# Reordering the steps of a hand-scheduled Mamba-2 decoder layer: conv tile one ahead of the gate, decays multiplied a step later

## The reference, cut to what matters

```python
proj = jnp.einsum('bsd,od->bso', h, in_proj_w)      # gate 8192, hid 8192, B 1024, C 1024, dt 128
hBC  = silu(causal_conv(hBC, conv_w, conv_b))        # 4 taps, on hid, B and C
...
Y_diag = einsum('bcijh,bcjhp->bcihp', (C.B) * L, hid*dt)   # L: exp of sums of A*dt, causal
y  = (Y_diag + Y_off) + D*hid
yg = y * silu(gate)
y  = yg * rsqrt(mean(yg*yg over the group) + EPS) * gnorm_w
out = residual + y @ out_proj_w.T
...
q1 = fake_quant(layernorm(x)); q2 = fake_quant(ctx); x = x + q1 @ q2
x = x + ffn(layernorm(x)[:, perm])[:, unperm]
```

## Time and profile before

| | us |
|---|---|
| median of 3 runs | 943.29 (942.54 to 943.3) |
| profiled execution, its own time | 941.07 |
| profiled execution, its span | 939.3 |
| PE busy | 821.1 (87%) |
| DVE busy | 696.5 (74%) |
| POOL busy | 624.8 (67%) |
| ACT busy | 542.9 (58%) |
| mean granted TensorE clock | 0.933 |

### The profile page before, as it was taken

One profiled execution on the slowest core, in us unless ns is written; L12 is line 12 of the kernel. 1 busy time (PEld: TensorE's weight loads), 2 busy tenths in 40 slices (PEclk: granted clock), 3 DMA queues, 4 the chain that ended last, 5 costly groups with the idle time before them and its releaser, 6 DMA issues.

```text
span 939.3 us, 14298 instructions
## 1 busy us (share of the span) xinstructions
PE 821.1 (87%) x4158; PEld 639.1 (68%) x4158; DVE 696.5 (74%) x912; ACT 542.9 (58%) x1124; POOL 624.8 (67%) x522
## 2 busy tenths in 40 slices
PE   4769898899989998999899998999899989994368
PEld 3547766677767776777677776777687767773155
DVE  6767578588958896797868895879589777672653
ACT  2357566465647664676656574666476665762253
POOL 3578999666856776576756785687667675767220
PEclk9889999899989998999989998999899999998579
DMA  5245344233434353433433343435243343300001
GB/s 189 90 152 201 115 145 146 90 135 123 150 100 147 108 169 107 145 131 126 145 109 133 112 148 134 134 106 172 79 145 134 127 142 124 116 31 22 1 0 45
DMA packets 44048, 111.11 MB, mean 118 GB/s; under 512 B 5748, under 2 KB 6644, under 8 KB 44020
## 3 DMA queue, kind: packets, MB, share of 16 engines
q1 hardware_dynamic: 44020, 110.76, 35.3%
HBM read 109.30 MB, written 1.44 MB: 118 GB/s over the span
## 4 chain that ended last, share of the span: by engine, by line
PE 45%; DVE 27%; issue 13%; ACT 7%; POOL 6%; DVEq 1%; DMA 0%; ACTq 0%; SPq 0%; POOLq 0%
PE ps_in L1147 9%; PE ps_in L1148 8%; PE ps_in L1149 8%; DVE hid L873 6%; PE ps_o L1147 4%; PE ps_o L1148 3%; PE ps_o L1149 3%; DVE z L956 3%; PE ps_y L1256 3%; DVE e L926 3%; DVE hdt L900 2%; DVE z L953 2%; ACT hid L611 2%; DVE bc L882 2%; PE ps_t L1217 1%
## 5 line engine op out<-in xcount | busy, mean ns | idle before, releaser
L1147 PE MATMUL ps_in<-h_hi,w_hi 128*128 128x512 f32 x560 | 232.2, 415 | 22.4 <-DVE gate L892 11.9
L1148 PE MATMUL ps_in<-h_lo,w_hi 128*128 128x512 f32 x560 | 228.4, 408 | 0.0
L1149 PE MATMUL ps_in<-h_hi,w_lo 128*128 128x512 f32 x560 | 227.8, 407 | 0.0
L462 POOL TENSOR_TENSOR wo_lo<-rawo,wo_hi 128x512 fp32r<-128x512 f32 x64 | 112.8, 1763 | 151.1 <-ACT wo_hi L599 97.5
L873 DVE SCALAR_TENSOR_TENSOR hid<-ps_in,curc,hid 128x510 f32<-128x510 f32 x186 | 138.9, 747 | 93.6 <-ACT hid L611 88.5
L452 POOL TENSOR_TENSOR w_lo<-raw,w_hi 128x512 fp32r<-128x512 f32 x144 | 188.9, 1332 | 15.7 <-ACT w_hi L591 15.6
L639 ACT ACTIVATE e<-e,nag 128x256 f32<-128x256 f32 (+1 forms) x512 | 183.6, 443 | 12.0 <-POOL e L472 12.0
L1147 PEld LDWEIGHTS ps_in<-h_hi,w_hi 128*128 128x128 f32 x560 | 111.2, 199 | 50.4 <-issue 24.2
L611 ACT ACTIVATE hid<-ps_in,curc 128x512 f32<-128x512 f32 x62 | 48.1, 776 | 150.4 <-PE ps_in L1149 139.4
L1149 PEld LDWEIGHTS ps_in<-h_hi,w_lo 128*128 128x128 f32 x560 | 111.4, 199 | 24.7
L1148 PEld LDWEIGHTS ps_in<-h_lo,w_hi 128*128 128x128 f32 x560 | 111.7, 199 | 22.9
(11 more groups left out here) (209 smaller groups left out, 1275.2 us busy)
## 6 DMA issues: line engine op xcount, KB each, us to landing
e<-acs_rows SPq DMA_DIRECT2D x64, 768.0 KB, 4.4
raw<-in_w_in SPq DMA_DIRECT2D x144, 256.0 KB, 4.7
rawo<-in_w_out SPq DMA_DIRECT2D x64, 256.0 KB, 2.6
craw<-in_ctx SPq DMA_DIRECT2D x8, 256.0 KB, 3.1
res<-in_x SPq DMA_DIRECT2D x4, 256.0 KB, 3.1
out_x<-res SPq DMA_DIRECT2D x4, 256.0 KB, 2.2
acs_rows<-z SPq DMA_DIRECT2D x3, 128.0 KB, 1.9
rawo<-in_w_dt SPq DMA_DIRECT2D x1, 256.0 KB, 4.3
```

Of the source, the lines that this page charges most:

```text
L462: pool.tensor_tensor(wo_lo[:, q % WO_RING, :], rawo[:, q % RAWO_RING, :], wo_hi[:, q % WO_RING, :].bitcast(F32), ALU.subtract).then_inc(s_ ...
L1147: pe.matmul(dst, lh, rh, start=first, stop=False)
L1148: pe.matmul(dst, lh, rl, start=False, stop=False)
L1149: return pe.matmul(dst, ll, rh, start=False, stop=last)
```

## The change

- Tile order: a step projects `h t` and then `g t-1` (with an extra tile between them), in place of `h t`, `g t`. The extras move from steps 3 and 5 to 4 and 6. The first C tile takes the place of the first gate.
- POOL and DVE multiply the decays of tile t-2 in step t (before: t-1), the same tile that PE's `outputs` takes in step t.
- ACT: `cast_out(t-2)` moves ahead of `tap0`; the casts of all tiles but the next `h` move to the end of the step, behind `z_high_and_square(t-2)`. POOL: the split of `g t` comes after `add_square`, then `mask_rows(t)`, `split_out(t-2)`, the second further tile, and then the next step's `decays_off(t-1)`.
- PE: `scores` moves from step 0 to step 1, `token_sums` from the front of step 2 to behind `out_tile`; DVE: `group_params` and `masked_scores` in step 1, `add_output` in step 3 between `decays_diagonal` and `turned`.
- The context moves from POOL in group 0 to DVE in group 7. The one-hot matrices move to DVE behind the last `mean_square`. The last square is not added on POOL but by PE.

```diff
 # tile order
 def step_tiles(n, t):
-    extra = {B_STEP: ["B"], C_STEP: ["C"]}.get(t, [])
-    return [("h", t), ("g", t)] + ([] if is_last(n) else [(x, t) for x in extra])
+    if t == CT:
+        return [(n, ("g", CT - 1))]
+    extra = extra_of(n, t)
+    back = (0, ("C0", 0)) if is_first(n) and t == 0 else (n, ("g", t - 1)) if t else (n - 1, ("g", CT - 1))
+    return [(n, ("h", t))] + ([(n, extra)] if extra else []) + [back]
+def following(n, t):
+    if is_last(n):
+        return step_tiles(n, t + 1) if t < CT else []
+    return step_tiles(n, t + 1) if t + 1 < CT else step_tiles(n + 1, 0)
...
 # POOL, step(n, t), as it is now for the groups of the loop
+                if t == 3 and not is_first(n):
+                    group_rms(n - 1)
+                if not lead:
+                    decays_off(*lagged(n, t, 2))
+                split_in(*tiles[0])
+                m, q = lagged(n, t, 3)
                 if q and not lead:
                     add_square(m, q)
+                    rows_arrived(n, t)
+                if len(tiles) > 1:
+                    split_in(*tiles[1])
+                    mask_rows(n, t)
+                    split_out(*lagged(n, t, 2))
+                if len(tiles) > 2:
+                    split_in(*tiles[2])
...
-            for k in range(DK):
-                pool.tensor_scalar(take[:, k, :], ...)
-                pool.tensor_scalar(put[:, k, :], ...)
             group_rms(last_m)
...
 # ACT, step(n, t)
+                    gate_tanh(*lagged(n, t, 2))
+                cast_in(*tiles[0])
+                if earlier:
+                    conv_tanh(n, earlier)
+                    cast_out(*lagged(n, t, 2))
                 tap0(n, ("h", t))
                     exps(*lagged(n, t, 1))
                 conv_tanh(n, ("h", t))
+                if extra:
+                    tap0(n, extra)
+                    z_high_and_square(*lagged(n, t, 2))
+                for tile in tiles[1:]:
+                    cast_in(*tile)
...
 # DVE, step(n, t)
+                    gated(*lagged(n, t, 2))
+                if t == 1 and not is_first(n):
+                    group_params(n)
+                    decays_diagonal(*lagged(n, t, 2))
+                if earlier:
+                    conv_silu(n, earlier)
+                if t == 3 and not is_first(n):
+                    dve.wait_ge(s_r, n)
+                    dve.wait_ge(s_ou, CT * n)
+                    for k in range(TT):
+                        add_output(k)
                     turned(*lagged(n, t, 1))
+                taps(n, ("h", t))
+                    skip_and_gate(*lagged(n, t, 2))
+                conv_silu(n, ("h", t))
+                    z_low(*lagged(n, t, 2))
+                if extra:
+                    taps(n, extra)
+                    masked_scores(n)        # step 1
+                    mean_square(n - 1)      # step 2
+                if is_last(n):
+                    context(t)
...
 # PE, step(n, t)
+                project(*tiles[0])
                     turn(*lagged(n, t, 1))
                     outputs(*lagged(n, t, 2))
+                for tile in tiles[1:-1]:
+                    project(*tile)
                     out_tile(*lagged(n, t, 3))
+                if t == 1 and not is_first(n):
+                    scores(n)
+                if t == 2 and not is_first(n):
+                    token_sums(n - 1)
+                project(*tiles[-1])
```

More of the change, by code:

```diff
@@ L370, in load_context, with store_acs @@
                   .then_inc(s_ctx[c % 2], 16)
-            def step(n, t):
[L373 to L378, removed]
+            def store_acs():
+                sp.wait_ge(s_dtv, 3)
+                for k in range(3):
+                    sp.dma_start(acs_dram[:, k, :, :], acs.rearrange("p (b c i) -> p c b i", b=BATCH, c=2)
+                                 [:, min(k, 1), :, :]).then_inc(s_acs, 16)
+                sp.wait_ge(s_acs, 16 * 3)
+                sp.wait_ge(s_res, TT)
+            def step(n, t):
                 if is_first(n):
@@ L512, in step @@
             def step(n, t):
-                if t == 2 and not is_first(n):
+                tiles = following(n, t)
+                lead = is_first(n) and t < 4
+                if t == 3 and not is_first(n):
                     group_rms(n - 1)
[L515 to L519, removed]
@@ L534, in step @@
-                if len(tiles) > 2:
-                    split_in(ahead[0], tiles[2])
+                if not lead:
+                    decays_off(*lagged(n, t, 2))
+                if is_first(n) and t == 3:
+                    decays_off(0, 0)
+                split_in(*tiles[0])
+                m, q = lagged(n, t, 3)
                 if q and not lead:
                     add_square(m, q)
[L538 to L542, removed]
@@ L544, in _ @@
-            for j in range(2):
-                split(j, j)
+                if not (is_first(n) and t < 2):
+                    rows_arrived(n, t)
+                    if is_first(n) and t == 2:
+                        rows_arrived(0, 0)
+                        rows_arrived(0, 1)
+                if len(tiles) > 1:
+                    split_in(*tiles[1])
+                if is_first(n) and t == 0:
+                    for k in range(TT):
+                        start_residual(k)
+                if is_first(n) and t == 2:
+                    mask_rows(0, 0)
+                    mask_rows(0, 1)
@@ L546, in _ @@
+                if not (is_first(n) and t < 2):
+                    mask_rows(n, t)
+                if not lead:
+                    split_out(*lagged(n, t, 2))
+                if len(tiles) > 2:
+                    split_in(*tiles[2])
+                if is_first(n) and t == 3:
+                    split_out(0, 0)
+                    decays_off(0, 1)
+                    split_out(0, 1)
+            split(0, 0)
             for tile in step_tiles(0, 0):
-                split_in(0, tile)
+                split_in(*tile)
@@ L1047, in _ @@
             mean_square(last_m)
+            for k in range(DK):
+                one_hot(k)
             def variance(tiles):
@@ L1291, in step @@
                 tiles = step_tiles(n, t)
-                lead = is_first(n) and t < 3
-                if t == 2 and not is_first(n):
-                    token_sums(n - 1)
-                project(n, tiles[0])
-                if is_first(n) and t == 1:
+                lead = is_first(n) and t < 4
+                project(*tiles[0])
+                if is_first(n) and t == 2:
                     dt_turn()
-                if is_first(n) and t == 2:
-                    scores(0)
+                if is_first(n) and t == 3:
                     turn(0, 0)
+                    turn(0, 1)
+                    outputs(0, 0)
                 if not lead:
@@ L1334, in _ @@
             last.then_inc(s_cq, 1)
[L1335 to L1337 removed]
+            last_token_sums()
             out_tile(last_m, CT - 1)
```

391 lines of the change are left out of this document (202 added, 189 removed).

## The result

| | before | after |
|---|---|---|
| median | 942.91 us (941.76 to 943.3, 4 runs) | 1030.19 us (1029.7 to 1032.59, 4 runs) |
| span of the profiled execution | 939.3 | 1030.9 |
| PE busy | 821.1 (87%) | 840.8 (82%) |
| mean granted TensorE clock | 0.933 | 0.91 |

The ratio is 1.0933, 95% interval 1.0912 to 1.0953: 9% slower. The forecast was 1020, range 940 to 1060.

The account below looks back on a forecast made before the run. PE bound the kernel before; a cross-engine chain would after. Start +3, six groups +73 (113 each), last group +13, constants +1, tail -12: +78 on 941.07 gives 1019, with the median's 2.2 offset 1020; range 940 to 1060.

Parts of the forecast that it names:

- The chain: From each `outputs` to the next, through DVE, ACT and POOL: 11.4 us a plain step, against PE's own 10.27.
- The clock: Low PE clock behind three stalls a group of 4 us or longer: 3 x 1.3 = 3.9 us more.
- lucky turns: DVE wins the port in three places where POOL was let first: 1.2 us each, a group at best 108.
- Step 3: `outputs` of step 3 to 4: four `add_output`, turned and taps delay z, plus an extra tile's split: 16.6 us.
- Step 2: `outputs` of step 2 to 3: `group_rms` on POOL adds 1.0, making 12.4 us.
- The start: Start until `outputs` of (0,4): first residual on POOL holds back splits and first rows: +3 us, bounds -4 and +8.
- the signs: New profile: some 60 waits of `outputs` for decays, longest in steps 4 and 6; POOL waits some 2 us a step.
- The last group: (7,2) to (7,7), with context on DVE filling idle time at 0.5 over 11.4 a step: +13 us, bounds +5 and +17.
- The tail: End of kernel: one-hots take 3.4 on DVE, last `outputs` loses its 5.71 wait: -12 us, bounds -8 and -18.
- The first rival: Port does not bite, DVE's and POOL's pieces fit each other's gaps: group 99.6 or some 102, whole 931 to 945; chance 0.10.
- PE's pace: Rival: cast and POOL's run fit into 10.27 a step, group falls to 90.1, whole about 868; chance 0.10.
- The harsh case: Rival: low clock feeds on itself, each slow `outputs` lengthening the next stall: above 1060 us; chance 0.05.

Follow-up runs that it names:

- experiment 1: On the changed kernel, ACT casts the next step's gate and extra tiles right behind cast_out, ahead of tap0: 933.99 us.
- experiment 6: On the changed kernel, PE does 24, 24 and 18 identity transposes ahead of its wait in steps 4, 6 and 0: 1002.04 us.
- experiment 3: On the changed kernel, further casts ahead of tap0 and POOL's decays_off a tile earlier, both at once: 931.77 us.
- experiment 5: On the changed kernel, DVE's decays_diagonal moved ahead of gated: 973.9 us.
- experiment 10: On the kernel before, context alone moved from POOL in group 0 to DVE in group 7: 947.03 us.
- experiment 8: Changed kernel with decays_off a tile earlier, decays_diagonal ahead of gated, and two of three context instructions cut to 16 of 512 columns: 885.32 us.
- experiment 7: On the changed kernel, decays_off a tile earlier and decays_diagonal ahead of gated, late casts kept: 887.32 us.
- experiment 2: On the changed kernel, POOL's decays_off one tile earlier, except a group's first tile; late cast kept: 910.77 us.
- two parts alone: On the kernel before, token sums moved behind out_tile and one-hots moved to DVE behind the last mean_square: 896.96 us.

## Why the prediction was right, and where its terms were off

**The chain.** Its links and their order are those of the prediction. It does not hold everywhere: before `outputs` of steps 5 and 7 PE waits for nothing in any of the six groups, so the stretches from step 4 to 5 and from 6 to 7 are PE's own 13.0 and up to 2.3 of low clock. Each cut of a different link gave a gain: the cast (96 us), POOL's decays (119), DVE's place for the other decays (56), DVE's share of them (84). They overlap, so they don't add. The Trainium skill, SBUF — State Buffer, section Who interferes with whom, has DVE and GpSimd share a port pair under a lock. The trace agrees where DVE's product of two SBUF tiles meets POOL's work: 2.12 against 1.22 here, and 2.01 in the mean of experiment 1.

**Step by step**, for the group from (4,2) to (5,2); each column is named by the step in which the stretch starts:

| from step | 2 | 3 | 4 | 5 | 6 | 7 | 0 | 1 |
|---|---|---|---|---|---|---|---|---|
| predicted, without clock | 12.4 | 16.6 | 13.4 | 15.6 | 13.4 | 14.4 | 12.8 | 12.5 |
| measured | 13.8 | 14.7 | 15.4 | 15.1 | 15.5 | 13.9 | 13.8 | 12.3 |
| mean of six groups | 13.8 | 14.8 | 15.1 | 15.1 | 15.3 | 13.9 | 14.5 | 12.7 |

The sum is 114.5 here and 115.0 in the mean. The prediction had 111.1 and 3.9 of clock, 115.0, and took 2 off again for lucky turns. That its own sum meets the mean to the tenth is luck, for three terms were mis-sized and cancel in part:

- *The clock.* I took 1.3 for each long stall and called the slow extra tile an upper case. It is the rule: steps 4 and 6 lose 2.0 and 2.1, and step 0 loses 1.0 of its 1.3. That is 5.1 a group, 31 us in six, near the 30.9 that experiment 6 took out of the six groups.
- *Step 3.* I let all four `add_output` lie behind `decays_diagonal` and so behind `outputs`, 16.6. But `outputs` waited for `decays_off`, which ended 1.2 after DVE had begun with `add_output`, so half of that lay before `outputs`:

```profile
537.70 2.73 DVE L1039 SCALAR_TENSOR_TENSOR res<-ps_o,rgrp,res 128x512 f32<-128x512 f32 x4 [0.92 <-POOL rgrp L547]
```

With `outputs` at 539.17, this is 14.7: 1.9 less.

- *Step 2.* POOL's root took 2.01 (535.65 to 537.66), not 1.0, and stood ahead of `decays_off` on POOL: 13.8 instead of 12.4. It is the port again, the prediction's own mechanism, left out of this term: the root was issued while `decays_diagonal` ran, which ended at 536.78, and was done 0.88 after it. In the loop of after it is so each time, 2.00 to 2.01; in experiments 3 and 5 the root's median is 1.02.

```profile
534.77 2.01 DVE L993 TENSOR_TENSOR e<-e,gm 128x1024 f32<-128x1024 f32 x1
535.65 2.01 POOL L547 TENSOR_TENSOR rgrp<-ssum,half 128x4 f32<-128x4 f32 x1
```

Steps 5 and 7 saved 0.5 each and step 1 0.2. So 111.1 + 5.1 - 1.9 + 1.4 - 1.0 - 0.2 makes the 114.5.

**The start** cost 6.5 instead of 3 and won 2.6 behind it: +3.9 in all, inside the bounds.

**The bounds and the signs.** The range 971 to 1060 is narrower than its terms: all low they add up to 966, all high to 1074, and no reason is given for the difference. Of the signs, some 60 waits of `outputs` were 49, and 36 of them for decays; the longest stand in steps 6 (4.7) and 0 (3.5), and in step 4 (2.8 to 4.4). POOL's wait for the cast was to be some 2 us a step. It is 2.8 in the last group's plain steps but 5.6 in the mean: the sign was worked out for the plain step alone, and steps with an extra tile or `add_output` bring z, and so the cast, later.

**The last group** came at +11.3 for +13. Its plain steps took 11.5 to 11.6 beside the 11.9 assumed. Here the context mostly filled DVE's idle time before `gated`: in step (7,6) its three instructions take 0.54, 1.46 and 0.74, and 0.55 of idle time is still left behind them. The prediction's 1.3 a step was for a DVE without such idle time. Of that, experiment 10 shows 0.8, and experiment 8 shows 0.3 to 0.6 for two of the three instructions.

**The tail** gave 8.7 of 12. Behind the last sums everything came as computed: the eight one-hots take 3.2 in all, and from the sums' scaling to the first `add_output` it is 3.3 where it was 12.25. But the other part, the wait of 5.71, was not won: from (7,7) to the last `outputs` it is 19.9 in both, because another wait took its place:

```profile
943.23 0.65 PE L1336 MATMUL ps_y<-e,hdt 128*64 128x256 f32 x4 [3.61 <-DVE e L993]
```

DVE was at the last tile's context from 938.02 to 941.40, with `gated` and `decays_diagonal` behind it. So this wait is at least in part a cost of the context, which the prediction had nowhere in its tail. No run shows it in after alone; experiment 8, with two of the three instructions cut short, takes 1.1 off the same stretch of experiment 7.

**The rivals.** The first rival left the port off the path, with a group of 99.6. In after it was on it: `decays_diagonal` takes 1.83 in the mean against 1.22 undisturbed. Experiment 2 is below that rival's figure (95.6) by its order, not by a port that doesn't bite, for there the same product still takes 1.63 in the mean. PE's pace, 90.1 a group, is within reach (92.5 in experiment 7) but only with both decays out of the way. The harsh case, above 1060, was not far: the six groups would have had to take 120 each.

**What I had wrong beyond the forecast.** Before experiment 1 I held the late cast to be the fault. Experiments 2 and 3 show that the fault is the pair, a late cast with `decays_off` behind its split; with `decays_off` out of the way, the late cast is worth 21 us (14 us at the least, since experiment 2 is a single execution and experiment 3 runs from 925.25 to 933.89).

## What to carry to other kernels

Before you put a wait into a step, write down the chain from the bottleneck's instruction in one step to the same one in the next, across all engines, and compare its length with the engine's own time: here that gave 111.1 us a group before any clock loss, against 90.1 of PE's own work and the 100.8 of before, and so the slowdown. Work made a step ahead is slack, and "just in time" takes it away; test the parts of such a rework one by one, for here two parts alone give -46 us and the whole gives +87. Where two engines share a port, an order that keeps them apart in time can beat one that starts both as soon as possible.

## What the runs showed of the hardware that I had not expected

- POOL's root of a 128x4 tile shows 1.02 us undisturbed and 2.01 when it is issued 0.88 behind the start of `decays_diagonal` on DVE: a tiny instruction waits for DVE's product like a large one.
- A tensor_scalar of 128x512 takes 0.42 on DVE alone and 1.09 to 1.40 beside a busy POOL (experiment 10). A copy of 128x64 took 0.38 and, beside `decays_off`, 1.33.
- Running POOL earlier made DVE's work longer by 8.6 us a group and the kernel slower by 21 us (experiments 2 and 3).
- Transposes whose results nobody reads gave 28 us back: the granted clock rose from 0.91 to 0.947 (experiment 6).
